# Two PSUM banks in turn for the heads' output sums, shared with the projections and output products

## What is computed

```python
qkv = jnp.einsum('bte,fe->btf', x, Wqkv)            # 8 heads, 64 each of q, k, v
q = q + pe; k = k + pe                              # the position table
scores = jnp.einsum('bhtd,bhsd->bhts', q, k) / sqrt(D)
probs = softmax(where(causal, scores, -inf))
attn = jnp.einsum('bhts,bhsd->bhtd', probs, v)      # the heads' outputs
out = jnp.einsum('btf,ef->bte', attn, Wo)
x = layernorm(x + out)
```

## Time and profile before

| | |
|---|---|
| median of three runs | 733.39 us |
| the profiled execution, its own time | 734.77 us |
| its span, first to last instruction | 733.0 us |
| mean granted TensorE clock in it | 0.967 of 2.4 GHz |
| PE busy | 654.5 us (89% of the span) |
| DVE, ACT, POOL busy | 504.9, 449.2, 503.1 us |
| attention, first sum of head 0 to the last of head 7 | 56.4 to 531.3 us |

### The profile page before, as it was taken

The page is one execution under the profiler, slowest core; times in us unless marked ns, Lnnn a source line. Parts: engine busy times, 40 slices in busy tenths (PEclk is TensorE's granted clock), DMA queues, the critical chain, the costliest instruction groups (busy, mean ns, idle before and its releaser), DMA issues. The chain is left out here.

```text
span 733.0 us, 10119 instructions
## 1 busy us (share of the span) xinstructions
PE 654.5 (89%) x3215; PEld 497.5 (68%) x3215; DVE 504.9 (69%) x1048; ACT 449.2 (61%) x626; POOL 503.1 (69%) x289
## 2 busy tenths in 40 slices
PE   5789999999999999999999999999877899989873
PEld 4557777777777777777677777777667687666651
DVE  3577667667766766866776676674187978877684
ACT  3436666676666666667667666667636577756551
POOL 6016887887878788788787778879943456667560
PEclk9979999999999999999999999999988899999995
DMA  7423211222112221122211232103300000000000
GB/s 186 110 64 70 61 44 45 46 69 60 44 43 49 69 58 44 44 51 69 55 44 44 53 71 51 45 1 91 98 2 1 0 1 1 0 16 0 14 1 29
DMA packets 27460, 33.75 MB, mean 46 GB/s; under 512 B 6897, under 2 KB 13842, under 8 KB 27282
## 3 DMA queue, kind: packets, MB, share of 16 engines
q1 hardware_dynamic: 27410, 33.14, 19.0%
HBM read 6.84 MB, written 1.05 MB: 11 GB/s over the span
## 5 line engine op out<-in xcount | busy, mean ns | idle before, releaser
L313 POOL TENSOR_TENSOR probs_l<-probs,probs_h 128x1024 fp32r<-128x1024 f32 (+1 forms) x160 | 347.5, 2177 | 132.0 <-PE o_ps L536 73.6
L407 DVE TENSOR_REDUCE m_part<-max_ps 128x1 f32<-128x512 f32 (+2 forms) x320 | 181.0, 605 | 111.0 <-PE max_ps L483 79.6
L350 ACT ACTIVATE probs<-scores 128x1024 f32<-128x1024 f32 (+1 forms) x160 | 150.3, 940 | 153.9 <-PE scores L511 96.7
L536 PE MATMUL o_ps<-probs_h,v 128*128 128x512 f32 (+5 forms) x640 | 185.2, 373 | 24.6 <-DVE oh L386 24.1
L353 ACT ACTIVATE probs_h<-scores 128x1024 fp32r<-128x1024 f32 (+1 forms) x160 | 149.8, 936 | 0.0
L536 PEld LDWEIGHTS o_ps<-probs_h,v 128*128 128x128 f32 (+1 forms) x640 | 95.9, 162 | 48.3 <-issue 20.0
L814 POOL TENSOR_TENSOR hid_lo<-hid,hid_hi 128x512 fp32r<-128x512 f32 x64 | 86.6, 1359 | 55.0 <-ACT hid_hi L894 42.3
L510 PE MATMUL scores<-q,k 128*128 128x512 f32 (+1 forms) x320 | 122.8, 384 | 0.0
L511 PE MATMUL scores<-q,k 128*128 128x512 f32 (+1 forms) x320 | 116.9, 365 | 0.0
L536 PE MATMUL o_ps<-probs_l,v 128*128 128x512 f32 (+1 forms) x320 | 116.4, 364 | 0.0
L483 PE MATMUL max_ps<-k,q 128*128 128x512 f32 (+2 forms) x320 | 103.1, 398 | 7.4 <-DVE m_part L407 6.2
(11 more groups left out here) (195 smaller groups left out, 986.9 us busy)
## 6 DMA issues: line engine op xcount, KB each, us to landing
k<-qk SPq DMA_DIRECT2D x96, 128.0 KB, 2.3
q<-qk SPq DMA_DIRECT2D x96, 128.0 KB, 2.3
q<-m_turn SPq DMA_DIRECT2D x128, 0.5 KB
v_all<-L_ffn_ew SPq DMA_DIRECT2D x2, 768.0 KB, 6.5
pos<-positions SPq DMA_DIRECT2D x1, 1024.0 KB, 6.8
out<-v_all SPq DMA_DIRECT2D x4, 256.0 KB, 2.3
acc<-L_attn_Wqkv SPq DMA_DIRECT2D x2, 256.0 KB, 3.9
v_all<-L_attn_Wo SPq DMA_DIRECT2D x2, 256.0 KB, 6.4
```

The lines of the kernel that those rows point to most:

```text
L313: pool.tensor_tensor(probs_l[:, p % 2, :, lo:CH], probs[:, p % 2, :, lo:CH], probs_h[:, n % 3, :, lo:CH], ALU.subtract).then_inc(S["probs_ ...
L350: act.activation(probs[:, p % 2, :, lo:CH], scores[:, p % 2, :, lo:CH], ACT.Exp, scale=D ** -0.5).then_inc(S["probs_ready"], 1)
L407: dve.tensor_reduce(m_part[:, r, j:j + 1], max_ps[:, u % 2, 0:width], AX.X, ALU.max).then_inc(S["tile_max_ready"], 1)
L536: last = pe.matmul(o_ps[0:rows, lo:CH], v, pr, start=(p == PAIR0[c] and j == 0 and k == 0), stop=(p == PAIR0[c + 1] - 1 and j == 1 and k = ...
```

## The change

`o_ps` and `side_ps` become one tensor of two banks, `out_ps`. Chunk c of head h is summed in bank (4h+c) mod 2: chunks 0 and 2 in bank 0, chunks 1 and 3 in bank 1. A projection or output product goes into the bank that is not summed in during its slot (`bank_beside`). Every first use of a bank, by a sum, a projection or an output product, waits for what emptied that bank's last user (`take_bank`), in place of the two waits in `pv_pair` and of `side_bank`. The schedule, the order on each engine and all other instructions stay.

```diff
+def bank_in_turn(h, c):
+    return (h * NC + c) % 2
+
+def bank_beside(table, h, c):
+    (slot, ahead), = [(s, a) for s, (of, a) in table.items() if of == c]
+    pair = max((h - ahead) * NP + slot - 2, 0)
+    return 1 - bank_in_turn(pair // NP, chunk_of(PAIR0, pair % NP))
...
-        o_ps = psum("o_ps", [P, CH])
         max_ps = psum("max_ps", [P, 2, CH])
-        side_ps = psum("side_ps", [P, CH])
+        out_ps = psum("out_ps", [P, 2, CH])
+
+        def o_ps(h, c):
+            return out_ps[:, bank_in_turn(h, c), :]
+        def projected_ps(h, c):
+            return out_ps[:, bank_beside(PROJECT, h, c), :]
+        def output_ps(h, c):
+            return out_ps[:, bank_beside(OUTPUT, h, c), :]
...
+            held = {0: (), 1: ()}
+            def take_bank(b, *released):
+                for signal, value in held[b]:
+                    pe.wait_ge(S[signal], value)
+                held[b] = released
...
                 if p == PAIR0[c]:
                     if p == 0:
                         pe.wait_ge(S["v_low_ready"], 2 * (h + 1))
-                    wait(pe, S["sums_turned"], h * NC + c)
-                    wait(pe, S["head_out_low_ready"], h * NC + c)
+                    take_bank(bank_in_turn(h, c), ("sums_turned", h * NC + c + 1), ("head_out_low_ready", h * NC + c + 1))
...
-            side = []
-            def side_bank(evacuated, value):
-                if side:
-                    pe.wait_ge(S[side[0][0]], side[0][1])
-                side[:] = [(evacuated, value)]
...
                     for c, of in due(OUTPUT, p, 0, h):
-                        side_bank("output_scaled", of * NC + c + 1)
+                        take_bank(bank_beside(OUTPUT, of, c), ("output_scaled", of * NC + c + 1))
                         output(of, c)
                     for c, of in due(PROJECT, p, 0, h):
-                        side_bank("qk_low_ready", of * NC + c + 1)
+                        take_bank(bank_beside(PROJECT, of, c), ("qk_low_ready", of * NC + c + 1))
                         project(of, c)
```

More of the change, by code:

```diff
@@ L335, in section @@
                         wait(act, S["output_projected"], of * NC + c - 1)
-                        act.activation(oh[0:D, c % 2, :], o_ps[0:D, :], ACT.Copy).then_inc(S["head_out_high_ready"], 1)
+                        act.activation(oh[0:D, c % 2, :], o_ps(of, c)[0:D, :], ACT.Copy).then_inc(S["head_out_high_ready"], 1)
                     for c, of in due(PROJECT, p, 1, h):
@@ L341, in section @@
                         wait(act, S["score_operands_moved"], 32 * n)
-                        act.activation(qk_hi, side_ps[:], ACT.Copy).then_inc(S["qk_high_ready"], 1)
+                        act.activation(qk_hi, projected_ps(of, c), ACT.Copy).then_inc(S["qk_high_ready"], 1)
                     if 0 <= h < H:
@@ L382, in section @@
                         dve.wait_ge(S["pv_done"], of * NP + PAIR0[c + 1])
-                        dve.transpose(l_rows[sums, c % 2, :], o_ps[sums, :]).then_inc(S["sums_turned"], 1)
+                        dve.transpose(l_rows[sums, c % 2, :], o_ps(of, c)[sums, :]).then_inc(S["sums_turned"], 1)
                         dve.wait_ge(S["head_out_high_ready"], n + 1)
                         wait(dve, S["output_projected"], n - 1)
-                        dve.tensor_tensor(oh[D:P, c % 2, :], o_ps[0:D, :], oh[0:D, c % 2, :], ALU.subtract).then_inc(S["head_out_low_ready"], 1)
+                        dve.tensor_tensor(oh[D:P, c % 2, :], o_ps(of, c)[0:D, :], oh[0:D, c % 2, :], ALU.subtract).then_inc(S["head_out_low_ready"], 1)
                     for c, of in due(PROJECT, p, 1, h):
@@ L391, in section @@
                         wait(dve, S["score_operands_moved"], 32 * n)
-                        dve.tensor_tensor(qk_lo, side_ps[:], qk_hi, ALU.subtract).then_inc(S["qk_low_ready"], 1)
+                        dve.tensor_tensor(qk_lo, projected_ps(of, c), qk_hi, ALU.subtract).then_inc(S["qk_low_ready"], 1)
                     for c, of in due(DONE, p, 1, h):
@@ L420, in section @@
                         wait(dve, S["output_added"], n)
-                        dve.tensor_tensor(scaled[:], side_ps[:], l_rows[:, c % 2, :], ALU.mult).then_inc(S["output_scaled"], 1)
+                        dve.tensor_tensor(scaled[:], output_ps(of, c), l_rows[:, c % 2, :], ALU.mult).then_inc(S["output_scaled"], 1)
                     for c, of in due(PROJECT, p, 0, h):
                         dve.wait_ge(S["qk_projected"], of * NC + c + 1)
-                        dve.tensor_tensor(side_ps[:], side_ps[:], pos[:, c * CH:(c + 1) * CH], ALU.add).then_inc(S["qk_positioned"], 1)
+                        dve.tensor_tensor(projected_ps(of, c), projected_ps(of, c), pos[:, c * CH:(c + 1) * CH], ALU.add).then_inc(S["qk_positioned"], 1)
                     if p in V_LOW and 0 <= h + 1 < H:
@@ L471, in project @@
                 for k, (w, a) in enumerate(((wth, xh), (wth, xl), (wtl, xh))):
-                    last = pe.matmul(side_ps[:], w[:, h, :, :].rearrange("p s d -> p (s d)"), a[:, xs], start=(k == 0), stop=(k == 2))
+                    last = pe.matmul(projected_ps(h, c), w[:, h, :, :].rearrange("p s d -> p (s d)"), a[:, xs], start=(k == 0), stop=(k == 2))
                 last.then_inc(S["qk_projected"], 1)
@@ L490, in output @@
                 for part, w in enumerate((woh, wol)):
-                    last = pe.matmul(side_ps[:], w[:, h, :], oh[:, c % 2, :], start=(part == 0), stop=(part == 1))
+                    last = pe.matmul(output_ps(h, c), w[:, h, :], oh[:, c % 2, :], start=(part == 0), stop=(part == 1))
                 last.then_inc(S["output_projected"], 1)
@@ L535, in pv_pair @@
                                                        (hi_v, P, probs_l[:, p % 2, j, lo:CH]))):
-                        last = pe.matmul(o_ps[0:rows, lo:CH], v, pr, start=(p == PAIR0[c] and j == 0 and k == 0),
+                        last = pe.matmul(o_ps(h, c)[0:rows, lo:CH], v, pr, start=(p == PAIR0[c] and j == 0 and k == 0),
                                          stop=(p == PAIR0[c + 1] - 1 and j == 1 and k == 2))
                 last.then_inc(S["pv_done"], 1)
-            side = []
-            def side_bank(evacuated, value):
-                if side:
-                    pe.wait_ge(S[side[0][0]], side[0][1])
-                side[:] = [(evacuated, value)]
             def section(h):
```

## The result

Four runs of the changed kernel beside four of the one before, on the same chip: 705.51 us median (702.18 to 706.70) against 733.12 us (732.24 to 735.25). The ratio is 0.9614, with a 95% interval of 0.9586 to 0.9642: 3.9% faster, 27.6 us. On another chip it was 705.67 us (five runs, 704.92 to 706.51) against 732.88 (eleven runs), ratio 0.9625 (0.9604 to 0.9646). Forecast were 706.5 us, 703 to 714.

The account below looks back on a forecast made before the run. PE, busiest engine, was taken to bound the attention, waiting for DVE's L386 before sums. 30.0 us, less 1.88 and 0.64 in head 7 and 0.1 in six heads, gives 26.9: 733.4 - 26.9 = 706.5 us, range 703 to 714.

Parts of the forecast that it names:

- The removed term: PE's 31 waits for DVE's L386 before chunk sums: 24.1 us shown, 30.0 us in all, the most the change can give.
- The addition of 0.19: us added to each PE wait's shown idle time, because a matmul counts as busy until its last result is out.
- Regular heads: Heads 1 to 6: each loses 3.79 us to four waits and keeps nearly all; 0.1 us taken off.
- What is late next: Releases PE reaches 0.8 to 1.2 us earlier: POOL's `probs_l` (margins 0.45, 0.1), maximum tiles (near 0, over 0.5).
- Head 7: POOL bounds its end: chunk 3's 1.88 us wait is worth 0, chunk 2's 0.89 about 0.25.
- The sum: 30.0 us, less 1.88 and 0.64 in head 7, less 0.1 in each of six heads: 26.9 us won.
- The clock: TensorE's clock expected to stay at 1.00 (2.4 GHz) over the heads, by the rows and against the skill's rule.
- 1: Part returns as PE waits for DVE's reductions or POOL: 0.4 us at some 27 waits, 11 us, 717; chance 0.10.
- 2: Nothing won: DVE's block L383 to L400 sets the pace, the wait moves one slot on; 731 to 733; chance 0.04.
- 3: Slower: chunk 2's sum waits for L421, deciding from 0.7 us of delay; 747 at 5 us a head; chance 0.02.
- 4: Clock falls for part of the attention; a fourth of it at half clock takes 119 us more, 826; chance 0.02.
- 5: The change doesn't do what it says: a chunk still waits for the chunk just before; 733; chance 0.02.

## Why the prediction was right

- **The removed term.** 31 waits of 24.1 us plus 0.19 each were to be worth 30.0 us at most. All 31 are gone, and putting them back took the whole gain away. The addition of 0.19 was right to 0.01 (1.34 us lost for 1.14 shown).
- **Regular heads.** Forecast 3.69 us a head, measured 60.94 - 57.20 = 3.74. From head 0's first sum to head 7's it was 425.13 us and is 399.16: 25.97 won, where the forecast's 26.9 less head 7's 1.1 gives 25.8.
- **What is late next.** No place cost anything: L503 never waits for L427, and the waits for POOL are all in head 7. The 0.1 us that I took off each head was hardly needed. The margins were 0.02 where "near 0" stood and 0.57 where 0.7 stood. In the changed kernel L441 ends at 240.64 and the sum starts at 241.37, as forecast, but the prediction left out the 0.15 us that pass from the end of DVE's operation to PE's start.
- **Head 7.** Behind its first sum 1.37 us were won (49.42 to 48.05), forecast 1.11 (0.86 for chunk 1, 0.25 for chunk 2). POOL bounds it as forecast. Its last seven pieces start 32.97 us behind the head's first sum in the kernel before and 31.77 in the changed one, 1.20 less, and take 15.53 us in place of 15.71, which the forecast did not have.
- **The sum.** 25.8 + 1.1 = 26.9 forecast, 25.97 + 1.37 = 27.34 measured. The predicted 706.5 was 1.0 us over the measured median, 0.4 of it in this sum; the rest is less than the runs of one kernel differ by (702.18 to 706.70), so it is partly luck that forecast and median lie this close.
- **The clock.** It stayed at 1.00 from 62 to 500 us with two banks in turn, and PE was busy in 57.20 of 57.20 us of a head. By the rule of the Trainium skill ("TensorE: Matmul & The Clock Gate", "A second HAM failure mode: psum-queue depth-cycling") time would have been lost; the trace speaks against it here. What the page describes, PE idle for moments between groups, is what the second bank took away.
- **The rivals.** 1: the mechanism exists (the added operation in slot 3 brought it out), but not without help. 2: no wait moved on. 3: decides from 0.6 us on, and made a kernel of 748 us when three additions took 4.09 us, its mechanism and the clock together. 4: not in this kernel; in the attention the clock fell only behind waits of 1.80 us and above, in kernels that had them put back or added. 5: the change does what it says.

The prediction missed one thing that did not matter for the number. It gave chunk 3's wait in head 7 the worth 0, which holds at full clock. In two kernels that wait was followed by a lower clock; alone it cost 1.7 us.

## What to carry to other kernels

An accumulator that is emptied while the engine that fills it waits is worth a second bank, even where that bank must be shared with side products: find who uses the idle one in each slot, and check that each new release has more margin than the time won ahead of it. Price a wait of PE by the distance of starts, not by the idle time shown, and measure a margin by adding one operation of known length; a margin read between the end of one engine's operation and the start of the other's still holds the time that the release takes, 0.15 us here. Where a queue has several waits ahead of an instruction, put last the one that is likely to block.

## What the runs showed of the hardware

**DVE held up by GpSimd.** The added DVE operation with both inputs in SBUF took 0.68 us with no GpSimd piece beside it, 1.56 beside a piece of POOL's in slot 3 and up to 2.87 in slot 7. The Trainium skill ("SBUF — State Buffer", "Who interferes with whom") says that a DVE instruction with two SBUF inputs contends with a GpSimd instruction that reads SBUF, and that the one issued second is held up. The runs agree, and give it a size: each time the added operation started while a piece of POOL's ran, it ended 0.55 us after that piece. In the kernel with one addition in slot 7 it started at 240.59, 0.15 us before a piece ended, and took 0.70; beside the last 1.0 us of a piece it took 1.56, beside nearly a whole one 2.87. The half low part of pair 19 took 1.66 us beside POOL's addition, again ending 0.55 after it, and 0.69 ahead of it. Transposes with one input took 0.67 us each in the middle of a piece. So the length of such a probe depends on where it falls, and has to be read from the trace.

**From DVE's end to PE's start.** In the kernels with operations added in slot 7, chunk 2's sum starts 0.15 us after the end of the scaling in every head.

**Waits in PE's queue.** Satisfied waits behind a blocked one cost 0.07 to 0.12 us, one or two alike.

**The clock after a gap.** Waits up to 1.17 us, 30 of them in the kernel with all put back, left the clock at 1.00 in the heads. The one of 1.69 to 1.80 us before chunk 3's sum in head 7 was followed by 0.66 and 0.72 over 5 us in two kernels, and by 1.00 in three. In the two, the clock was at 0.50 from 488.4 and from 490.2 us on, 0.3 and 1.5 us after the wait had ended, for 3.4 us each. The waits of 3.24 to 3.52 us in eight heads were followed by 0.50 in seven, and by 1.00 in head 7. What decides between the two is open.
